# A quantised residual adapter stack on one core: a unit's last selection and x1 ahead of the next unit's steps, first remainders of v and u later, w2's first remainders used later

## The reference, cut to what matters

```python
x = x + dequantised(x)          # 8 thresholds: the level's delta and zero point are picked by |x|, 0 above all of them
x = x + einsum('bsi,boi->bso', x, weight[itok_B_3_7])                         # W1: one 1024x1024 matrix per batch row
x = x + einsum('bsi,oi->bso', x, W) + 0.5 * low(x, lora_A[itok_B_0_2]) @ lora_B_w.T    # W2, shared, and rank 32
x = x + (x @ B[itok_B_3_7].T) @ A[itok_B_3_7].T                               # rank 16
```

## Time and profile before

| | us |
|---|---|
| median of 3 runs | 484.09 (483.89 to 484.51) |
| the profiled execution's own time | 483.97 |
| its span, from the first to the last instruction | 482.2 |
| TensorE matmuls busy | 465.1 |
| VectorE busy | 419.4 |
| ScalarE busy | 358.3 |
| GpSimd busy | 44.9 |

### The profile page before, as it was taken

The page is one execution under the profiler, slowest core; times in us unless marked ns, Lnnn a source line. Parts: engine busy times, 40 slices in busy tenths (PEclk is TensorE's granted clock), DMA queues, the critical chain, the costliest instruction groups (busy, mean ns, idle before and its releaser), DMA issues.

```text
span 482.2 us, 8216 instructions
## 1 busy us (share of the span) xinstructions
PE 465.1 (96%) x3184; PEld 425.0 (88%) x3184; DVE 419.4 (87%) x481; ACT 358.3 (74%) x383; POOL 44.9 (9%) x46
## 2 busy tenths in 40 slices
PE   3999869999999999999999999999999999999997
PEld 3969669898999989898999989898999989898995
DVE  5999999999999899989999899989999899989120
ACT  6969958678877879678887879678886879675011
POOL 1063001200002000110002000110003000110000
PEclk9999989999999999999999999999999999999999
DMA  7997214712335122712335122712335122702002
GB/s 278 411 416 255 114 34 149 294 45 104 132 113 226 43 87 104 294 43 103 130 107 230 44 86 105 294 43 103 131 98 239 43 85 105 294 2 88 1 1 87
DMA packets 17830, 67.07 MB, mean 139 GB/s; under 512 B 2576, under 2 KB 5904, under 8 KB 13712
## 3 DMA queue, kind: packets, MB, share of 16 engines
q1 hardware_dynamic: 17808, 66.81, 37.8%
HBM read 56.84 MB, written 9.96 MB: 139 GB/s over the span
## 4 chain that ended last, share of the span: by engine, by line
PE 86%; ACT 5%; SPq 3%; DMA 3%; DVE 2%; issue 1%; POOL 1%; DVEq 0%
PE x_bank L604 45%; PE acc L629 34%; PE x_bank L617 3%; DMA w1b<-w 3%; PE acc L641 2%; PE acc L639 2%; ACT mask L343 1%; ACT tq L328 1%; ACT w2h L399 1%; DVE y L459 1%; SPq L197 1%; SPq L196 1%; SPq L206 0%; SPq L216 0%; POOL w1b L294 0%
## 5 line engine op out<-in xcount | busy, mean ns | idle before, releaser
L604 PEld LDWEIGHTS x_bank<-x,w1b 128*128 128x128 f32 x2048 | 233.2, 193 | 8.1 <-issue 5.0
L604 PE MATMUL x_bank<-x,w1b 128*128 128x128 f32 x2048 | 234.8, 276 | 3.7 <-DVE x L474 3.7
L343 ACT ACTIVATE mask<-absx,negtop 128x1024 bf16<-128x1024 f32 x112 | 128.4, 1146 | 40.2 <-DVE y L459 39.5
L328 ACT ACTIVATE tq<-xin,magic,rdelta 128x1024 f32<-128x1024 f32 x128 | 156.9, 1234 | 0.6 <-DVE yhigh L527 0.3
L459 DVE COPY_PREDICATED y<-mask,uq 128x1024 f32<-128x1024 int16 x112 | 150.4, 1343 | 0.1
L438 DVE TENSOR_SCALAR tq<-tq,par 128x1024 f32<-128x1024 f32 x128 | 98.0, 766 | 3.7 <-DVE y L459 3.1
L447 DVE TENSOR_SCALAR uq<-tq,ylow,yhigh 128x1024 f32<-128x1024 f32 x112 | 93.2, 832 | 0.2 <-DVE y L459 0.2
L629 PE MATMUL acc<-w2h,x2h 128*128 128x512 f32 x256 | 80.9, 393 | 2.3 <-DVE x2l L480 2.3
L629 PE MATMUL acc<-w2h,x2l 128*128 128x512 f32 x256 | 79.9, 390 | 0.0
L629 PE MATMUL acc<-w2l,x2h 128*128 128x512 f32 x256 | 79.2, 390 | 0.0
L294 POOL TENSOR_TENSOR w1b<-w1b,eye 128x256 f32<-128x256 f32 x32 | 36.1, 1130 | 370.4 <-DMA w1b<-w 370.4
(11 more groups left out here) (57 smaller groups left out, 218.9 us busy)
## 6 DMA issues: line engine op xcount, KB each, us to landing
w1b<-w SPq DMA_DIRECT2D x32, 1024.0 KB, 6.7
xin<-x SPq DMA_DIRECT2D x16, 512.0 KB, 3.7
out<-outb SPq DMA_DIRECT2D x14, 512.0 KB, 2.8
w2g<-w2n SPq DMA_DIRECT2D x4, 1024.0 KB, 10.4
ring<-w2t SPq DMA_DIRECT2D x6, 512.0 KB, 10.0
ua<-e_dram SPq DMA_DIRECT2D x16, 128.0 KB, 2.5
ua<-w2t SPq DMA_DIRECT2D x2, 512.0 KB, 9.6
va<-la SPq DMA_DIRECT2D x8, 128.0 KB, 2.7
```

The costliest lines, as they stand in the source:

```text
L328: nc.scalar.activation(tq[:, n % TQ, :], flat(xin, c % UN), ACT.Identity, bias=magic[:, 0:1], scale=rdelta[:, g:g + 1]).then_inc(t_ready, 1)
L343: nc.scalar.activation(mask[:, n % MK, :], absx[:, :], ACT.Relu, bias=negtop[:, g:g + 1], scale=1.0).then_inc(mask_ready, 1)
L604: last = nc.tensor.matmul(x2_bank[2 * t + i][:, o % HALF * P:(o % HALF + 1) * P], w1b[:, o, at:at + P], x1[:, t, k, :], start=(o % HALF == ...
```

## The change

Four edits. In the step that ends a unit, VectorE now issues select, cut and x1 first, and the next unit's value and clamp behind them. v's first remainder moves from step 15 to 18 and u's from step 23 to 26, for the first batch row only. TensorE's first four LOW products wait for a count of selections. U_AT goes from 3 to 4. ScalarE's and SyncE's programs are the same instruction for instruction.

```diff
-        ACT_V, DVE_V = 14, 15
-        ACT_U, DVE_U = 21, 23
+        ACT_V, DVE_V, DVE_V0 = 14, 15, 18
+        ACT_U, DVE_U, DVE_U0 = 21, 23, 26
...
                 dve.wait_ge(y_cut, c + 1)
-                if G * (c + 1) < STEPS:
-                    clamp(G * (c + 1))
                 if c == 1:
                     dve.wait_ge(g_out, 16)
...
-                    if s == DVE_V:
+                    if s == (DVE_V if b else DVE_V0):
                         split_v(b)
-                    if s == DVE_U:
+                    if s == (DVE_U if b else DVE_U0):
                         split_u(b)
...
                 if ends_unit:
                     await_selection(n - 2)
+                    select(n - 2)
+                    close_unit(n // G - 1)
                 if n < STEPS:
                     value(n)
+                if ends_unit and n < STEPS:
+                    clamp(n - 1)
...
-                if 2 <= n < STEPS + 2:
+                if not ends_unit and 2 <= n < STEPS + 2:
                     select(n - 2)
-                if ends_unit:
-                    close_unit(n // G - 1)
...
-            U_AT = 3
+            U_AT = 4
...
                 if first:
+                    pe.wait_ge(y_ready, selections(2 * G - 1))
                     for k in range(HALF):
                         pe.wait_ge(w2l_ready, k + 1)
                         product(0, k, LOW)
```

## The result

The changed kernel takes 489.45 us, median of 5 runs (489.28 to 490.63), against 484.09 (5 runs, 483.85 to 484.51) before: a ratio of 1.0118, 95% interval 1.0107 to 1.0129. The forecast was 489.3.

What follows compares the result with a forecast made beforehand. TensorE, busy 96% of the span, was taken as the bound, with its second unit's w1_x1 start and later waits fixing the end. 483.97 + 4.5 (u) + 1.9 (clock) - 1.1 (later units) = 489.3 us, range 487.5 to 491.6.

Steps and rivals of the forecast that it cites:

- What decides: u at step 26: First batch row: later u_hl delays W1's pairs in SyncE's list; TensorE idles 7.5 us, o = 2 starts 4.5 us later.
- The 8.8 us from u_hl's end to the pair's readiness: From u_hl's end to GpSimd's add on pair one done: 8.79 and 8.75 us in two rows, taken as 8.8.
- a bound downwards only (1.1 us less): GpSimd's add took 1.85 and 1.54 us there but 0.73 elsewhere, so 1.1 us less at best.
- The formula for one transfer: For a 1 MB pair of W1: about 2.0 us plus bytes over 436 GB/s, 4.4 us against the trace's 4.81.
- The clock behind the wait: After TensorE's 7.5 us of idle time ahead of o = 2, the low clock costs 1.9 us.
- The rival with 3.76 us: Behind TensorE's wait the low clock lasts longer, costing 3.76 instead of 1.87 us: 491.2 us, chance 0.14.
- x1 first, LOW held back: Unit two: x1 ends 1.40 us earlier, LOW products split the idle time, clock stays up for another 1.87 us.
- The assumption that the clock stays up after 2.3 us of idle time: Idle time of 2.27 us at 54 to 56.5 was followed by clock 1.00, so the clock was taken as kept.
- Later units: x1 comes 1.4 us earlier relative to TensorE; 0.18 us at six second units goes: -1.1 us.
- v at step 18, U_AT = 4: Moving v's 0.53 us out of step 15 gives nothing there; U_AT moves eight matmuls and changes no count.
- The faster rival: W1's pairs don't stand in the way; TensorE's row one starts 3.0 us earlier: 479.9 us, chance 0.05.
- 88.7: Time before which u_hl must end for the faster rival: 97.5 - 8.8 us, 7.5 us sooner than predicted.

Runs made afterwards that it cites:

- e2: Kernel before with one edit, u's first remainder at step 26 for the first batch row: 490.75 us, ratio 1.0135.
- e1: Changed kernel with u's first remainder back at step 23: 481.51 us, ratio 0.9943 to the kernel before.
- e3: Changed kernel with SyncE's wait for ul_ready and load_u moved behind the four W1 pairs: 480.66 us, ratio 0.9927 to the kernel before.
- e5: Changed kernel with u's first remainder at step 25 instead of 26: 489.94 us, ratio 1.0122 to the kernel before.
- e11: Changed kernel with u's first remainder at step 24, without any pause: 481.16 us, ratio 0.9943 to the kernel before.
- e10: Changed kernel with one VectorE pause ahead of step 29's value, for pair one's add: 489.62 us, ratio 1.0127 to the kernel before.
- e4: Kernel before with one edit, select, cut and x1 ahead of the next unit's value and clamp: 481.26 us, ratio 0.9936.
- e7: As e3, without the wait ahead of TensorE's four LOW products: 480.93 us, ratio 0.9932 to the kernel before.
- e8: As e3, with v's first remainder back at step 15: 480.31 us, ratio 0.9922 to the kernel before.
- e12: Changed kernel with U_AT back at 3: 489.83 us, ratio 1.0121 to the kernel before.
- e9: As e5, with three VectorE pauses ahead of the values of steps 27, 28 and 29: 481.79 us, ratio 0.9959 to the kernel before.

## Why the prediction was right, by its own steps

**What decides: u at step 26.** Right in mechanism and place. e2 brings the loss with this edit alone, e1 and e3 take it away by its place on VectorE or by SyncE's list. Predicted and measured: u_hl's end 96.2 and 96.4; the issue of the pairs 98.3 and 98.56; pair one ready 105.0 and 105.40; TensorE's wait 7.5 and 7.71.

**The 8.8 us from u_hl's end to the pair's readiness.** The size was right for this kernel, the term was not what I took it for. I took two rows of before that agreed as one duration. It is a sum of SyncE's issues and the transfer (2.1 and 4.8 to 5.0 us in all these traces, counted to the start of the add) and of an add that took 0.72 to 7.14 us by what VectorE did beside it. In the changed kernel it came to 9.0 us because VectorE ran dry 1.4 us after the pair had landed; that the add's 1.97 us lie near the 1.85 of before is luck. In e5 the same reasoning gave 481.5 to 482.3, and 489.94 was measured. For the add I had a bound downwards only (1.1 us less) and none upwards. The Trainium skill, "SBUF — State Buffer", section "Who interferes with whom", says that GpSimd and VectorE share one pair of SBUF ports, held by one of them at a time, and that this is the only contention between engines. The lengths agree with that in kind, on both sides: 0.73 us alone and up to 7.14 beside VectorE for the add, 0.81 becoming 1.22 for a clamp (e11). That the loser stays out over some ten instructions of the winner, as in e5, the traces show and the section doesn't say. The formula for one transfer that the prediction takes from the Trainium skill stands in a section on GpSimd's queue, as its title says; W1's pairs are issued by SyncE, and 4.81 us was measured in the changed kernel too.

**The clock behind the wait.** Right in kind; the size was too small for the profiled execution: 2.6 us instead of 1.9. The low level began inside the wait, was there at its end, and lasted for about 3 us (e2), 4.9 us (the changed kernel) and 5.8 us (e10) of work. The rival with 3.76 us was too much. In the profiled execution the sum is thus 1.15 us short (0.45 at o = 2, 0.7 for the clock); that 489.3 falls within 0.2 us of the median is in part luck, since the runs next to the median lost less than the profiled one. Between the runs this is the likeliest cause of the spread of 1.35 us, since those of 489.3 to 489.5 have a mean granted clock of 0.992 or 0.993 and the two above 490 have 0.990; it was not tested by itself.

**x1 first, LOW held back.** x1 of unit two ended at 64.50 (64.46 predicted), w1_x1 began at 64.65 (64.60), with its clock at 1.00. That the gain would be swallowed by the later wait was right: e3 and e4 show it where the wait is absent. The assumption that the clock stays up after 2.3 us of idle time, taken from one row, held for some executions and not for others (e7), and in e8 the clock fell after 1.81 us at the very place of that row. The length of the idle time alone does not decide it. Behind the split idle time of 1.42 and 0.56 us it stayed up in the trace of after, and in all runs of e1 the mean is 0.999 or 1.000.

**Later units.** -1.1 us, as measured: all second units from 131.52 to 456.52 take 14.29 us in the chain, and the 7.5 us by which the first of them starts later (131.52 against 124.04) are 6.5 at the last (456.52 against 450.06).

**v at step 18, U_AT = 4.** v was said to give nothing at step 15, which is right, but at step 18 it costs about 0.35 once the large wait is away (e8). U_AT costs and gives nothing that e12 could tell.

**The faster rival.** Its point of decision, u_hl done before 88.7 us, is not borne out as a fixed time. At step 24 it ends at 88.03 and the kernel is faster than before; at step 25 it ends at 90.55 and the kernel is slower (e5), but with the add let through it ends at 90.50 and the kernel is faster (e9). The 88.7 came from the 8.8 us, and so from the add's length.

## What to carry to other kernels

An instruction that is moved later on its own engine moves everything that waits for it in another engine's list, and what stands behind that wait in the list too. Ask what the queue behind the waiting transfer is for: here the tile u itself was not urgent, three transfers behind it were. And where the price of a hand-over is read from a row, read its parts; a part that depends on what runs beside it is not a constant, even where two rows agree.

The best version found is e8 (x1 first, LOW held back, W1's pairs ahead of load_u, u at 26, v at 15): 480.31 us, 0.8% under the kernel before.

## What the runs showed of the hardware that I had not expected

GpSimd's add on 128x256 values took 0.72 to 0.73 us while VectorE stood and 7.14 us beside an unbroken run of VectorE's instructions (the profiled execution of e5, whose four times lie within 0.6 us). A wait of 0.66 us on VectorE let it through at once, and with this and the two other pauses the kernel was about 8 us faster (e9). In four kernels the add ended 0.58 to 0.59 us after VectorE had run dry (e2, e5, e12, the changed kernel).

The clock fell behind an idle time of 1.81 us in one execution (e8) and stayed up behind one of 2.27 us at the same place in another (before). After a long wait the low level lasted for 3 to 5.8 us of work (e2, e10).
